# First attention of a perceiver block: the gathered values transposed by DMA instead of TensorE, a unit later

## What is computed

```python
def _L0_xattn_ref(inputs_q, inputs_kv, Wq, Wk, Wv, Wo):       # H, HD = 16, 128
    q = (inputs_q @ Wq).reshape(b, sq, H, HD) * (1.0 / np.sqrt(HD))
    k = (inputs_kv @ Wk).reshape(b, skv, H, HD)
    v = (inputs_kv @ Wv).reshape(b, skv, H, HD)
    attn = jax.nn.softmax(jnp.einsum('bqhd,bkhd->bhqk', q, k), axis=-1)
    ctx = jnp.einsum('bhqk,bkhd->bqhd', attn, v).reshape(b, sq, H * HD)
    return ctx @ Wo
x = x + _L0_xattn_ref(_layernorm(x), ctx_2048, ...)   # first attention: the change is here
x = x + _L0_attn_ref(_layernorm(x), ...)              # "mix": cosine mixing with rotary K, V
x = x + _L0_ffn_ref(_layernorm(x), ...)               # "experts": top 2 of 8
x = x + _L1_xattn_ref(_layernorm(x), ctx_2048, ...)   # second attention, 8-bit quantized
x = x + _L1_attn_ref(_layernorm(x))                   # "dilated"
x = x + _L1_ffn_ref(_layernorm(x), ...)               # "feed": MX-quantized weights
```

## Time and profile before

| | us |
|---|---|
| median of 3 runs | 747.83 (747.34 to 754.0) |
| the profiled execution | 750.32 |
| its span, first to last instruction | 749.0 |
| TensorE busy | 670.9 (90%) |
| VectorE busy | 575.8 (77%) |
| ScalarE busy | 371.3 (50%) |
| GpSimd busy | 198.6 (27%) |
| first attention, first scores to the second attention's first | 22.1 to 497.6 |
| mean granted clock of TensorE | 0.958 |

### The profile page before, as it was taken

The page is one execution under the profiler, slowest core; times in us unless marked ns, Lnnn a source line. Parts: engine busy times, 40 slices in busy tenths (PEclk is TensorE's granted clock), DMA queues, the critical chain, the costliest instruction groups (busy, mean ns, idle before and its releaser), DMA issues. The chain is left out here.

```text
span 749.0 us, 13021 instructions
## 1 busy us (share of the span) xinstructions
PE 670.9 (90%) x4894; PEld 426.0 (57%) x4894; DVE 575.8 (77%) x1069; ACT 371.3 (50%) x584; POOL 198.6 (27%) x315
## 2 busy tenths in 40 slices
PE   4899999999999999799899999979998988879743
PEld 3456676667666767476566667744553444334431
DVE  3698876977776787677687776749989999999555
ACT  4553334333433443253334336318868998778711
POOL 3285333343334301240000000016324332223100
PEclk9999999999999999899999999989999999999855
DMA  8456965555555578566366475637977999888900
GB/s 285 122 136 145 205 135 126 129 122 118 124 130 122 119 152 232 115 177 167 84 143 182 115 142 131 151 139 136 187 144 142 189 198 177 141 131 158 171 1 7
DMA packets 330639, 107.29 MB, mean 143 GB/s; under 512 B 297032, under 2 KB 328016, under 8 KB 330320
## 3 DMA queue, kind: packets, MB, share of 16 engines
q1 hardware_dynamic: 330576, 106.45, 66.6%
HBM read 32.23 MB, written 0.26 MB: 43 GB/s over the span
## 5 line engine op out<-in xcount | busy, mean ns | idle before, releaser
L804 PE MATMUL psum<-c_nat,eT 128*128 128x256 f16 x1536 | 190.7, 275 | 0.0
L1487 ACT ACTIVATE cT<-psum,bias,q_scale 128x1024 f16<-128x1024 f32 x128 | 153.5, 1203 | 39.7 <-PE psum L1412 33.7
L778 PE MATMUL psum<-cT,qk 128*128 128x512 f16 x768 | 171.0, 379 | 1.2 <-ACT cT L715 1.1
L804 PEld LDWEIGHTS psum<-c_nat,eT 128*128 128x128 f16 x1536 | 152.0, 99 | 26.5 <-issue 0.3
L1412 PE MATMUL psum<-kT,v_space 128*128 128x512 f16 x512 | 144.5, 391 | 20.1 <-DVE tops L1518 15.9
L1518 DVE TENSOR_REDUCE tops<-psum 128x1 f32<-128x512 f32 x256 | 158.1, 679 | 2.4 <-PE psum L1412 2.2
L778 PEld LDWEIGHTS psum<-cT,qk 128*128 128x128 f16 x768 | 74.9, 98 | 86.1 <-ACT cT L715 1.3
L927 DVE TENSOR_REDUCE neg_max<-psum 128x1 f32<-128x2048 f32 x32 | 73.3, 2290 | 33.3 <-PE psum L778 33.1
L1412 PEld LDWEIGHTS psum<-kT,v_space 128*128 128x128 f16 x512 | 45.6, 99 | 91.5 <-DVE tops L1518 61.9
L915 DVE TENSOR_TENSOR e_lo<-e_all,e_hi 128x2048 f16<-128x2048 f32 x32 | 77.5, 2422 | 0.0
L890 ACT ACTIVATE e_all<-psum,neg_max 128x2048 f32<-128x2048 f32 x32 | 63.1, 1973 | 11.3 <-DVE neg_max L929 11.3
(11 more groups left out here) (224 smaller groups left out, 796.2 us busy)
## 6 DMA issues: line engine op xcount, KB each, us to landing
wq_h<-in_L_xattn_Wq SPq DMA_DIRECT2D x32, 128.0 KB, 2.2
wk_h<-in_wkT SPq DMA_DIRECT2D x32, 128.0 KB, 2.2
wv_h<-in_L_xattn_Wv SPq DMA_DIRECT2D x32, 128.0 KB, 2.2
wo_h<-in_L_xattn_Wo SPq DMA_DIRECT2D x32, 128.0 KB, 2.2
mx_land<-in_mx_weights SPq DMA_DIRECT2D x8, 384.0 KB, 3.5
v_space<-in_ctx SPq DMA_DIRECT2D x4, 512.0 KB, 7.4
cT<-in_ctx SPq DMA_DIRECT2D x2, 1024.0 KB, 11.1
c_nat<-in_expert_wT SPq DMA_DIRECT2D x2, 1024.0 KB, 5.9
```

The lines of the kernel that those rows point to most:

```text
L778: ins = pe.matmul(s_ps[:, n * 512:(n + 1) * 512], c.qk[:, u % 2, q_part, k, :], m.cT[:, b, c_part, 4 * n:4 * n + 4, k, :], start=(k, q_par ...
L804: ins = pe.matmul(u_ps, c.eT[:, v % 2, e_part, j, :], m.c_nat[:, v // H0, c_part, j, :], start=(j, e_part, c_part) == (0, 0, 0), stop=(j, ...
L1487: act.activation(x.y[:, u % 2, q * CHUNK:(q + 1) * CHUNK], m.bank(3 + 2 * (q % 2), 2), ACT.Exp, bias=x.bias[:, u:u + 1], scale=m.q_scale[: ...
```

## The change

The fp32 transposes of `u_sb` on TensorE are left to the last two heads. For the 30 others ScalarE copies `u_sb` to fp16, GpSimd subtracts to get the remainder, SyncE issues one DMA transpose of both parts (128 x 512), and GpSimd adds the transposed parts to `uT_sb`. The value product and the output product of these heads are made in iteration w + 4 instead of w + 3; Wv and Wo get a third buffer. Since batch 0's heads are complete a unit later, all side stages move by one unit (`xT` of the mixing by one unit and one slot). GpSimd's side stages are now woven into `pool_cross`. 1 / sum is made ahead of the second key tile and the folded key. The transposes of batch 1's context are issued in four groups, in units 4 to 7, behind the key tiles, instead of both at once in unit 4 ahead of `e_hi`. The last two heads are turned, multiplied and added inside one iteration each.

```diff
+TURNED = UNITS - 2
-MIX_AT = dict(norm=(18, 2), again=(18, 3), scaled=(19, 0), plus=(19, 1), xT=(19, 2), qkv0=(20, 0), qkv1=(20, 2),
-              turn=(20, 3), squares=(21, 0), product=(21, 1), unit=(21, 2), a=(22, 0), yT=(22, 2), out=(23, 0))
-EX_AT = dict(norm=(23, 0), apply=(23, 1), xT=(23, 2), gate=(24, 0), gap=(24, 2), coef=(24, 2), prod0=(24, 3),
-             prod1=(25, 1), prod2=(26, 1), prod3=(26, 3), coefT=(27, 0), bias=(27, 1))
+MIX_AT = dict(norm=(19, 2), again=(19, 3), scaled=(20, 0), plus=(20, 1), xT=(20, 3), qkv0=(21, 0), qkv1=(21, 2),
+              turn=(21, 3), squares=(22, 0), product=(22, 1), unit=(22, 2), a=(23, 0), yT=(23, 2), out=(24, 0))
+EX_AT = dict(norm=(24, 0), apply=(24, 1), xT=(24, 2), gate=(25, 0), gap=(25, 2), coef=(25, 2), prod0=(25, 3),
+             prod1=(26, 1), prod2=(27, 1), prod3=(27, 3), coefT=(28, 0), bias=(28, 1))
...
 def sp_cross(sp, m, c, d, g, s, t):
...
             sp.dma_start_transpose(c.eT[:, v % 2, 1], c.e_lo[:, :]).then_inc(s[f"lo_turned{v % 2}"], 16)
+            sp_turn_values(sp, c, s, v - 2)
...
+        if 4 <= u < 4 + GROUPS:
+            tiles = slice((u - 4) * GROUP, (u - 3) * GROUP)
+            sp.wait_ge(s["late_hi"], 2)
+            sp.wait_ge(s["late_lo"], 2)
+            for part in range(2):
+                sp.dma_start_transpose(m.cT[:, 1, part, tiles].rearrange("p t k s -> p (t k) s"),
+                                       flat(m.c_nat[:, 1, part, tiles])).then_inc(s["late_turned"], 16)
...
+def sp_turn_values(sp, c, s, v):
+    if 0 <= v < TURNED:
+        if v > 0:
+            sp.wait_ge(s["uT_out"], v)
+        sp.wait_ge(s["u_lo"], v + 1)
+        sp.dma_start_transpose(c.uT_parts.rearrange("p a k q -> p (a k) q"), flat(c.u_parts)).then_inc(
+            s[f"u_turned{v % 2}"], 16)
...
+def pool_turned_values(pool, c, s, w):
+    if 0 <= w < TURNED:
+        pool.wait_ge(s[f"u_turned{w % 2}"], 16 * (w // 2 + 1))
+        if w > 1:
+            pool.wait_ge(s["oT"], w - 1)
+        pool.tensor_tensor(flat(c.uT_sb[:, w % 2]), flat(c.uT_parts[:, 0]), flat(c.uT_parts[:, 1]), ALU.add).then_inc(
+            s["uT_out"], 1)
...
+def pool_cross(pool, m, c, d, s, side):
+    for u in range(UNITS + 3):
+        w = u - 3
+        if 0 <= w < TURNED:
+            pool.wait_ge(s["u_hi"], w + 1)
+            if w > 0:
+                pool.wait_ge(s[f"u_turned{(w - 1) % 2}"], 16 * ((w - 1) // 2 + 1))
+            pool.tensor_tensor(c.u_parts[:, 1, :], c.u_sb[:, :], c.u_parts[:, 0, :], ALU.subtract).then_inc(s["u_lo"], 1)
+        side.upto(4 * u + 1)
...
+            if kt % 2 == 0:
+                pool_turned_values(pool, c, s, w)
+        if u >= H0:
+            pool_turned_values(pool, c, s, w)
+        side.upto(4 * u + 3)
...
+def turned_due(u):
+    return u - 4 if 0 <= u - 4 < TURNED else None
+def last_due(u):
+    return u - 3 if TURNED <= u - 3 < UNITS else None
...
 def pe_cross(pe, m, c, d, g, s, side):
...
-        if w >= 0:
-            pe.wait_ge(s["u_out"], w + 1)
-            if w > 0:
-                pe.wait_ge(s["added"], w)
-            for k in range(KD):
-                ins = pe.transpose(o_ps[:, k * P:(k + 1) * P], c.u_sb[:, k * P:(k + 1) * P], m.ident[:, :])
-            ins.then_inc(s["uT"], 1)
...
+        w, last = turned_due(u), last_due(u)
+        if w is not None:
             pe.wait_ge(s["uT_out"], w + 1)
+            value_product(w)
+            if last is not None:
+                output_product(w)
         if 0 <= v < UNITS:
             attend(v, 1)
+        if last is not None:
+            turn_values(last)
...
 def act_cross(act, m, c, s, side):
...
             act.mul(c.u_sb[:, :], u_ps, c.inv_sum[:, :]).then_inc(s["u_out"], 1)
+            if v < TURNED:
+                act.wait_ge(s["u_out"], v + 1)
+                if v > 0:
+                    act.wait_ge(s[f"u_turned{(v - 1) % 2}"], 16 * ((v - 1) // 2 + 1))
+                act.copy(c.u_parts[:, 0, :], c.u_sb[:, :]).then_inc(s["u_hi"], 1)
```

More of the change, by code:

```diff
@@ L73 @@
     late_hi late_lo late_turned
-    scores raw_max max exp e_hi e_lo hi_turned0 hi_turned1 lo_turned0 lo_turned1 pv inv_sum u_out uT uT_out oT oT_out
+    scores raw_max max exp e_hi e_lo hi_turned0 hi_turned1 lo_turned0 lo_turned1 pv inv_sum u_out u_hi u_lo u_turned0 u_turned1 uT_out uT uT_copied oT oT_out
     head_out added
@@ L524, in sp_cross @@
         if 4 <= u <= UNITS + 1:
-            sp.wait_ge(s["head_out"], u - 3)
+            if u > 4:
+                sp.wait_ge(s["head_out"], u - 4)
             sp_load_output(sp, c, s, t, u - 2)
[L527 to L532, removed]
         if 0 < u <= UNITS:
@@ L788, in keys_values @@
         if kt == KTB:
-            pe.wait_ge(s["late_turned"], 32)
+            pe.wait_ge(s["late_turned"], 32 * GROUPS)
         for k in range(KD):
@@ L807, in attend, with turn_values, value_product, output_product @@
             ins.then_inc(s["pv"], 1)
+    def turn_values(w):
+        pe.wait_ge(s["u_out"], w + 1)
+        pe.wait_ge(s["added"], w)
+        for k in range(KD):
+            ins = pe.transpose(o_ps[:, k * P:(k + 1) * P], c.u_sb[:, k * P:(k + 1) * P], m.ident[:, :])
+        ins.then_inc(s["uT"], 1)
+    def value_product(w):
+        if w > 0:
+            pe.wait_ge(s["added"], w)
+        pe.wait_ge(s[f"wvo_in{w % 3}"], 32 * (w // 3 + 1))
+        for k in range(KD):
+            ins = pe.matmul(o_ps[:, D:D + P], c.wv_h[:, w % 3, k, :], c.uT_sb[:, w % 2, k, :], start=k == 0,
+                            stop=k == KD - 1)
+        ins.then_inc(s["oT"], 1)
+    def output_product(w):
+        pe.wait_ge(s["oT_out"], w + 1)
+        pe.matmul(o_ps[:, 0:D], c.oT_sb[:, :], c.wo_h[:, w % 3, :], start=True, stop=True).then_inc(s["head_out"], 1)
     for u in range(UNITS + 3):
-        v, w = u - 2, u - 3
+        v = u - 2
         if u < UNITS:
@@ L851, in pe_cross @@
         side.upto(4 * u + 3)
[L852 to L855, removed]
+        if last is not None:
+            pe.wait_ge(s["uT_copied"], last - TURNED + 1)
+            value_product(last)
+        elif w is not None:
+            output_product(w)
         if u < H0:
@@ L859, in pe_cross, with turned_out @@
             attend(v, 3)
+        if last is not None:
+            output_product(last)
 def act_cross(act, m, c, s, side):
     s_ps, o_ps, u_ps = m.bank(0, 4), m.bank(6), m.bank(7)[:, 0:D]
+    def turned_out(w):
+        act.wait_ge(s["oT"], w + 1)
+        if w > 0:
+            act.wait_ge(s["head_out"], w)
+        act.copy(c.oT_sb[:, :], o_ps[:, D:D + P]).then_inc(s["oT_out"], 1)
     for u in range(UNITS + 3):
-        v, w = u - 2, u - 3
+        v, w, last = u - 2, turned_due(u), last_due(u)
         if u in (1, 2):
@@ L878, in act_cross @@
         side.upto(4 * u + 1)
[L879 to L883, removed]
+        if w is not None:
+            turned_out(w)
         if u < UNITS:
@@ L898, in act_cross @@
             act_fold_key(act, m, c, s, u + 2)
+        if last is not None:
+            act.wait_ge(s["uT"], last - TURNED + 1)
+            act.wait_ge(s["oT"], last - 1)
+            act.copy(flat(c.uT_sb[:, last % 2]), o_ps[:, 0:D]).then_inc(s["uT_copied"], 1)
+            turned_out(last)
         if 0 <= v < UNITS:
@@ L909, in dve_cross, with add_output @@
     s_ps, kv_ps, o_ps = m.bank(0, 4), m.bank(5), m.bank(6)
+    def add_output(w):
+        b = w // H0
+        dve.wait_ge(s["head_out"], w + 1)
+        dve.tensor_tensor(m.x_res[:, b, :], m.x_res[:, b, :], o_ps[:, 0:D], ALU.add).then_inc(s["added"], 1)
     def remainder(v):
@@ L942, in dve_cross @@
         side.upto(4 * u + 1)
[L943 to L950, removed]
+        if w is not None:
+            add_output(w)
         if 0 <= v < UNITS:
@@ L960, in dve_cross @@
         side.upto(4 * u + 3)
+        if last is not None:
+            add_output(last)
 def dve_key_tile(dve, m, d, s, kt):
```

55 lines of the change are left out of this document (25 added, 30 removed).

## The result

| | before | after |
|---|---|---|
| median of 20 runs each | 750.56 (745.71 to 755.10) | 755.68 (753.41 to 761.51) |
| ratio, 95% interval | | 1.0077 (1.0053 to 1.0101) |
| span of the profiled execution | 749.0 | 752.9 |
| units 0 to 15 | 229.47 | 225.73 |
| unit 16 to the second attention's first matmul | 246.03 | 258.34 |

The change makes the kernel 0.8% slower, and there are gains and losses of several microseconds behind it.

A forecast was written before the change was run, and what follows sets the result against it. TensorE bounds the first half; in the second, VectorE and behind it SyncE's queue make it wait. Stalls of +7.3 us with -6.6 for transposes give +0.7: median 748.5 us, own range 744 to 753, wide range 738 to 757.

The forecast's parts named there:

- slower, by the clock: Rival: stalls of 1.8 to 2.4 us in units 17, 20, 21, 23, 27 bring half clock; 756 to 760 us; chance 0.18.
- unit 17: Second half: the mx_land load lands later, so folded key and value scales are late for TensorE: +2.1 us.
- `xm`: unit 19 to 20: Mixing stage: unit 19's 4.6 stall and 3.0 slow clock go (-7.6); unit 20 waits until 12.8 (+2.4).
- unit 23: Second half: y ready 11.2 us into the unit, wanted at 9.1: +2.1.
- `xn`: unit 23 to 24: Experts: unit 23's old stall goes (-5.2); in unit 24 apply stands behind dve_slice_units, stall 6.5 plus slow clock 3.0 (+9.5).
- expert sum: unit 26 to 27: TensorE's wait for the expert sum moves a unit later, 2.3 before and 2.0 after: -0.3 us.
- small ones, GpSimd: Earlier small waits -0.2 us; GpSimd's added subtraction and addition slowing VectorE in the second half, +0.5.
- tail (0.88 come back, two transposes less): After unit 30: later reciprocal for head 29 (+1.6); iteration 33's value and output products with a copy between (+0.6).
- The queue: SyncE: a new DMA transpose each unit, 1.3 us of issue ahead of the mx_land load; VectorE's loop 25.9 becomes 27.2.
- no slow clock (as after 2.1): Unit 20: TensorE's wait of +2.4 us brings no half clock, since an earlier wait of 2.1 brought none.
- The queue delay is hidden and the shift pays: Rival: stalls of units 17, 21, 23 stay away, unit 24 costs 6.2; 739.2 us, 736.8 without unit 20's; chance 0.20.
- The stalls keep their sizes: Rival: stalls move but keep their old sizes, only TensorE's 6.6 us of work goes: 741.2 us; chance 0.10.

The follow-up runs named there:

- the fastest one: Changed kernel with apply in slot 0, mx_T transpose and mx_land load issued ahead of e_lo's transpose, six mixing-weight loads one iteration later: 731.22 us, 0.9760.

## Why the prediction was right, and where it wasn't

The median went up by 5.1 us, where the forecast was +0.7 (748.5 against 747.83). 755.68 is inside the wide range of 738 to 757 and within 1%, but above the forecast's own 744 to 753 and just under the 756 to 760 of "slower, by the clock". As a difference, since the kernel before came out at 750.56 and not 747.83, the 5.1 are at the upper edge of the first (+5.2) and short of the second (+8). In the profiled executions it is 3.9 (749.0 to 752.9). Step by step, in us, with 0.22 for each transpose taken out of a unit set against it in the row for units 16 to 30:

| | forecast | measured |
|---|---|---|
| units 0 to 15 (unit 3's 0.88 among it) | -3.7 | -3.74 |
| transposes out of units 16 to 30 | -3.3 | -3.3 |
| unit 17 | +2.1 | +2.6 |
| `xm`: unit 19 to 20 | -5.2 | -1.9 |
| unit 21 | +1.8 | +2.2 |
| unit 23 | +2.1 | +4.3 |
| `xn`: unit 23 to 24 | +4.3 | +2.0 |
| expert sum: unit 26 to 27 | -0.3 | +1.0 |
| small ones, GpSimd | +0.3 | +0.2 |
| tail (0.88 come back, two transposes less) | +2.6 | +5.2 |
| ahead of unit 0 | 0 | -0.9 |
| second attention to the end | 0 | -3.8 |
| sum | +0.7 | +3.9 |

*Right.* The price of a transpose on TensorE, 0.22 us, to the hundredth. The queue: the load is issued 1.3 us later behind `e_lo` in units 18 and 20, as forecast (in unit 24 `mx_amax` is 1.28 later, with only 0.82 of it from the queue, so there the number fits by chance), and a test of this cause alone, an issue that does nothing, costs 1.2% and 1.4% of the time in either set of places. The largest wait in unit 24, behind the slice units: 5.6 for the 6.5 of the forecast, between the 4.4 and 7 that were to show it. (That for `xm`, to be under 3, was 3.2.) The shift of the stages is worth something by itself, 0.9%, by the `xm` stall that it ends. And the four pieces are worth nothing in idle time.

*The step that failed: "no slow clock (as after 2.1)".* The forecast took the half clock to follow a wait by its size, from one 2.1 that hadn't brought it and one 3.4 that had. Units 17, 20 and 23 waited 2.0, 3.2 and 2.6 us (forecast 2.4 and 2.1 for the last two), and all three have a clock of 0.90, a tenth of about 17 us or 1.7 lost in each. That is 5.1 us, where their three rows of the table were short by 6.0. Unit 27 waited 2.6 us and shows 1.00 (and 0.92 behind the same 2.6 with `apply` in slot 0), and in the kernel with the pieces 3.4 us passed with 1.00 too. So size alone doesn't decide, here between 2.0 and 3.4. This is the rival "slower, by the clock": it came true in three places of its five, with 5.1 us where four were to give 7 to 12, and the `xn` stall gave some of it back: the wait was 0.9 shorter than forecast, and the clock of 0.92 in unit 24 is 1.6 us, where 3.0 were added.

*Unit 20, the other part.* `xm` was there 13.7 us into the unit, not 12.8. The timeline shows `e_hi` waiting 1.36 us for a transpose's DMA, and the folded key another 1.41 behind it; the forecast had nothing for the backlog that the mixing weights' loads leave on the queue. Splitting those loads, in a kernel with the early load, took the whole wait away; in the change itself it wasn't tried. GpSimd's two operations took 0.72 and 0.73, for 0.8.

*The tail.* The reciprocal of head 29 stands on VectorE behind a rounding of the last slice, as forecast, but TensorE waited 3.0 us (1.04 in the earlier trace rows) and not 2.6, then issued 12 matmuls in 2.7 us instead of 1.47, at the half clock, and waited 0.7 once more for a `u_sb`.

```profile
485.76 2.72 PE L851 MATMUL psum<-c_nat,eT 128*128 128x256 f16 x12 [3.04 <-ACT u_sb L974]
...
494.21 1.47 PE L851 MATMUL psum<-c_nat,eT 128*128 128x256 f16 x12 [0.66 <-ACT u_sb L974]
```

*What helped the number by chance.* The code behind the first attention is the same, and it is 3.8 us shorter in the profile. It is 247.6 to 250.0 us in the six kernels with the moved transposes, and 250.1 to 252.7 in the eight without them. Of the 3.8, 3.4 lie in one stretch of 280 matmuls near the end, before and after:

```profile
685.98:716.95 30.97, 23.84 (x280) 13.54 (x280) 19.81 (x37) 21.58 (x38) 5.25 (x16) 0.83 0.85 139
693.42:721.00 27.58, 23.15 (x280) 12.26 (x280) 19.55 (x36) 21.59 (x38) 5.30 (x16) 0.94 0.88 158
```

The clock is lower in the longer one. In the two kernels with the transpose that does nothing, which keep theirs on TensorE, the stretch is short too (28.7 and 28.8 us). Why the clock falls there in some kernels and not in others no run was made to find out, and it stays open. Without it, and the 0.9 us ahead of unit 0, the sum would have been 8.6: the forecast's nearness owes that much to luck.

*The rivals.* "The queue delay is hidden and the shift pays" fell as told, since the delay isn't hidden; but its second half was shown. With the delay mended alone the time is 751.74 us; only with `apply` moved too is it 741.86, near the 739.2 it gave. "The stalls keep their sizes" fell: they didn't.

## What to carry to other kernels

An engine's in-order queue is a resource like the engine: a transfer added to it delays whatever stands behind it, and 0.22 us saved on the bounding engine lost against 1.24 us of issue ahead of a load that other engines wait for. Before moving work to a queue, find the next thing behind it that is waited for, and put the new work after that; the same change with its issue there took 0.7% less, and 1.9% less once a stage, too, no longer stood behind that load. When stages of a schedule shift by an odd number of units, check which engine's periodic work now stands ahead of each.

## What the runs showed of the hardware

- The issue of a DMA transpose takes SyncE's queue 1.24 us (128x512), 1.6 (2048 columns of `e_lo`), and 5.47 for the same 2048 behind twelve loads; with six of the loads gone 3.63. The number of loads alone doesn't set it: behind the same twelve it was 4.65 in the kernel before, and 5.06 behind seven others in the fastest one.
- Half clock followed waits of 2.0, 2.6 and 3.2 us and did not follow others of 2.6 and 3.4; a wait of 2.6 in unit 27 left it at 1.00 in the change and at 0.92 with `apply` in slot 0; the same waits of 4.6 and 3.4 us left units 19 and 23 at 0.83 and 0.91 in one kernel and 0.91 and 1.00 in another.
- GpSimd's subtraction of 128x256 (L642) took 0.67 us in unit 20 and 2.58 beside VectorE's `e_lo` in unit 24, while that `e_lo` took 2.29. Nine times it began while `e_lo` ran: it took 1.65 to 2.67 and ended 0.53 us behind `e_lo` each time, and `e_lo` kept 2.27 to 2.29. Three times it began 0.49 us ahead of `e_lo`: it took 1.1, and `e_lo` 2.76. So GpSimd paid all of it in the nine, and about half in the three. Over all units `e_lo` rose from 2422 to 2494 ns in the mean, 2.3 us of VectorE in all. The Trainium skill ("GPSIMD Engine Reference", Specifications) has GpSimd contend with VectorE's instructions of two SBUF inputs: the trace agrees.
- The Trainium skill ("DMA: Bandwidth & Descriptors", Rules for kernel authors) advises to issue a DMA early and wait for it late. Issuing `mx_land` ahead of `e_lo`'s transpose took 23 us of waits from VectorE; it showed in the time of the kernel whose TensorE waited (0.9891 to 0.9800), and not in that of the one which didn't (0.9816 and 0.9822).
